# Pairs of units as one 1024-column product and one weighting, a third folded pair of quads, and a reordered prologue

## The chip, the cores and the metric

The kernel runs on one core of one Trainium2 chip. The metric is the device time of one execution in microseconds (us), the median of several runs. Engines are named as in the profile: PE (TensorE), DVE (VectorE), ACT (ScalarE), POOL (GpSimd) and SP (SyncE, which here only issues DMAs).

## The reference

x is 8 batches of 512 tokens of 256 features. Every batch goes through four layers in order, each adding to x:

- Layers 0 and 3: linear attention (16 and 8 heads) on a normalised x, with a softmax over the tokens for the keys and over a head's features for the queries; then y is normalised, scaled and shifted by the condition, passed through SiLU and projected.
- Layers 1 and 2: a state-space block on a normalised, modulated x, whose core is

```
def step(h, inp):
    dt_t, B_t, C_t, u_t = inp
    dA = jnp.exp(dt_t[:, :, None] * A)
    h = h * dA + (dt_t * u_t)[:, :, None] * B_t[:, None, :]
    y = jnp.einsum('bdn,bn->bd', h, C_t)
```

with 512 channels and 16 states for each channel, over 512 tokens. The result is multiplied by silu(z) and projected.

## The kernel before, in words

A **unit** is one state n of 128 channels: a scan along the 512 tokens, 128x512 elements. A scan (one batch, one of layers 1 and 2) has 4 chunks of 128 channels and 16 states, so 64 units, in two halves of 32: within a half the units run over n, and for each n over the half's two chunks. Those two successive units have the same row of B and the same row of C. There are 16 scans, so 1024 units.

A unit g consists of

- the decay exp(dt*A), by ACT;
- the injection dtu*B. For a unit of kind BESIDE, ACT writes the decay to one of three PSUM banks (L887) and POOL writes dtu*B into the unit's state slot (L664). For a unit of kind SPREAD, ACT writes the decay to SBUF (L903) and copies the row of B into a PSUM bank (L895), and DVE multiplies that bank by dtu in place (L1153);
- the scan on DVE (L1160 for BESIDE, L1163 for SPREAD), in place in one of 20 state slots. Before, unit g uses PSUM bank g % 3, free once unit g - 3 is scanned (`m_scan`);
- the weighting by the row of C on POOL, in place (L673, `weight`);
- the sum over n: PE adds the slot into a PSUM bank through the identity (L1463). Two of the eight quads (four units) of each half are not summed directly: an accumulating DMA issued by POOL (L677, `fold`) adds quad 0 into quad 1 and quad 3 into quad 4, and PE sums only the targets.

`KINDS` gives the kind: of 16 units, 7 are BESIDE. Rows of B and C come by DMA from SP into rings of four rows each, and a slot is free when the units that use it are done.

All engines walk one program order: a tick for each unit, in two parts, and in each part first the unit's own work and then as many steps of the chains (attention, the preparation of the next scan `before`, the work after a scan `after`, setup) as are due by hand-tuned tables of ticks (`ATT_STAGES`, `PREP_STAGES`, `POST_STAGES`, `TAIL_STAGES`, `SETUP_STAGES`). POOL also forms dtu = dt*u for each half of a scan (L629, 128x1024) and, by a power, the inverse roots of the norms (L605). Every engine works in order, so a chain's step that waits holds back the units behind it. Leads and lags in ticks: the row and the decay in a bank are made 2 ticks ahead, POOL's injection 3 ahead, the DVE product (L1153) 1 ahead of its scan, the weighting 2 behind, the sum 4 behind (12 for a folded quad).

Ahead of unit 0 lie the loads, attention 0, most of attention 1 and the preparation of scan 0. Among them the ACT queue waits, ahead of attention 0's normalisation, for the masks to have been stored to DRAM (L745), and DVE makes the masks and then the pieces of the biases (`bias_pieces`).

Of the kernel before, what the change touches and what calls it, by code (L numbers as in the profile page):

```python
# [34 lines left out]
KINDS = (BESIDE, SPREAD) * 7 + (SPREAD, SPREAD)  # L35
TAIL_UNITS, POST_END, PREP_END = 3, {1: 24, 2: 26}, 60
SETUP_UNITS, FIRST_PREP, FIRST_ATT = (-147, -66), (-79, -14), (-71, 34)
ATT_UNITS = ((32, 92), (93, 154), (154, 218), (218, 281))
# [25 lines left out]
MOD_PICK = 8 * DC + 2 * TT  # L64
MODS = MOD_PICK + 1
# [14 lines left out]
def by_name(names, durations):  # L80
# [4 lines left out]
    "first": (3, 19, 20, 20, 31, 13, 4, 6, 28, 4, 62, 1, 1, 2, 9, 13, 10, 15, 0, 2, 11, 15, 37, 4, 14, 6, 0, 2, 30,  # L85
              16, 10, 1, 18, 17, 29, 26, 34, 15, 65, 18, 9, 1, 11, 0, 10, 3, 12, 0, 20, 7, 4, 14),
    "second": (2, 1, 3, 2, 0, 4, 0, 3, 3, 4, 4, 2, 3, 3, 3, 0, 0, 4, 0, 2, 5, 14, 1, 22, 2, 0, 16, 3, 1, 0, 2, 0, 6,
# [9 lines left out]
    "last": (8, 7, 10, 2, 26, 4, 13, 17, 8, 24, 13, 58, 8, 11, 1, 12, 8, 4, 27, 33, 3, 6, 46, 2, 11, 1, 34, 2, 16, 11,  # L97
             12, 12, 5, 20, 5, 6, 6, 5, 60, 0, 20, 8, 12, 15, 5, 6, 22, 17, 4, 1, 3, 4),
})
PREP_STAGES = by_name(PREP_NAMES, {  # L100
    "first": (5, 9, 3, 1, 2, 3, 0, 4, 5, 3, 0, 4, 7, 4, 0, 1, 4, 5, 9, 1, 6, 9, 4, 9),
# [4 lines left out]
})  # L106
POST_STAGES = by_name(POST_NAMES, {
# [4 lines left out]
})  # L112
TAIL_STAGES = by_name(TAIL_NAMES, {
    0: (3, 14, 7),
    1: (0, 32, 4),
    2: (14, 7, 5),
    3: (34, 17, 9),
})
SETUP_STAGES = dict(zip(SETUP_NAMES, (0, 1, 1, 0, 15, 38, 1, 22, 3, 24, 3, 10), strict=True))
# [35 lines left out]

def kind_of(g):
    return KINDS[g % len(KINDS)]


def nth(g):  # L160

    kind = kind_of(g)
    return g // len(KINDS) * KINDS.count(kind) + KINDS[:g % len(KINDS) + 1].count(kind)
# [4 lines left out]

def spread_unit(n):
    return SPREAD_UNITS[n - 1]  # L170


def quad_of(g):
    return g // HALF_UNITS, g % HALF_UNITS // QUAD
# [154 lines left out]
def bass_cond_seq(nc, x, out, mask_cols, keep_cols, mask_rows0, mask_rows3, order, const_pack, att_packs, ssm_packs,  # L329
# [4 lines left out]
    with ctx:  # L334
# [583 lines left out]
        def _(dve):  # L918
# [112 lines left out]
            def attention(ai, layer, s, b):  # L1031
# [13 lines left out]
                if ai == 0:  # L1045
                    bias_pieces()
# [509 lines left out]
```

## Time and profile before

| | before |
|---|---|
| median of 3 runs | 2320.88 us (2319.4 to 2322.88) |
| profiled execution | 2320.92 us, span 2318.9 us |
| POOL busy | 2000.3 us (86%) |
| DVE busy | 1980.6 us (85%) |
| PE busy | 1931.7 us (83%) |
| ACT busy | 1691.9 us (73%) |
| mean granted clock | 0.928 |

Busy time is the union of an engine's instructions. Back-to-back records overlap by some 0.05 to 0.1 us, so what an instruction costs in a full queue is the distance from start to start, which is less than its mean duration. The share over the whole span mixes a prologue of 137 us, the 1024 units, and an end in which one attention runs alone.

### The profile page before, as it was taken

Reading aid. Unit: us, or ns where it says so; the run is one execution under the profiler, and the core shown is the slowest. Engines: PE = TensorE matmul, PEld = TensorE weight load, DVE = VectorE, ACT = ScalarE, POOL = GpSimd, SP = SyncE. Lnnn points to the kernel's source line nnn. Section 1 sums busy time; section 2 is a strip of 40 time slices with the busy share of each in tenths; the row PEclk is TensorE's granted clock in tenths of the full one; section 3 lists DMA queues with packets and bytes.
Section 4 is the critical chain, followed back from the end, with each engine's and each line's share of the span. In section 5 each row is a group of like instructions: output and inputs, shape, how many; then the busy total and the mean of one; then the engine's idle time right before and its main releaser. Section 6 shows DMA issues by size and latency. Waiting matters only on the chain. (4 is left out here: it accounts for less than half of the span.)

```text
span 2318.9 us, 23892 instructions
## 1 busy us (share of the span) xinstructions
PE 1931.7 (83%) x5712; PEld 984.9 (42%) x5712; DVE 1980.6 (85%) x2705; ACT 1691.9 (73%) x2677; POOL 2000.3 (86%) x1720
## 2 busy tenths in 40 slices
PE   6767779898888889889888979889898978778786
PEld 5433324445444444435444444435445443333353
DVE  4468888989989898998989898998989998898862
ACT  2476868697787869688787968778796867678642
POOL 0079998989899998999899998998999999999950
PEclk9887989899999999899999999999999999898997
DMA  6046565655455565555546565564556555565620
GB/s 229 1 135 170 157 181 143 181 155 161 145 166 167 153 191 155 164 166 153 159 143 180 160 178 158 159 174 142 160 157 180 163 157 180 161 175 162 173 77 19
DMA packets 170538, 358.84 MB, mean 155 GB/s; under 512 B 19528, under 2 KB 27936, under 8 KB 161696
## 3 DMA queue, kind: packets, MB, share of 16 engines
q1 hardware_dynamic: 151504, 275.38, 36.3%
q0 software_dynamic: 9216, 67.11, 15.5%
q10 hardware_dynamic: 9680, 14.83, 1.8%
q8 instruction: 47, 0.77, 0.1%
q14 instruction: 91, 0.75, 0.1%
HBM read 284.85 MB, written 5.29 MB: 125 GB/s over the span
## 5 line engine op out<-in xcount | busy, mean ns | idle before, releaser
L673 POOL TENSOR_TENSOR state<-state,c_rows 128x512 f32<-128x512 f32 x1024 | 1313.3, 1340 | 86.5 <-DVE state L1160 46.3
L1463 PE MATMUL bank<-state,const_sb 128*128 128x512 f32 x1536 | 766.7, 617 | 84.9 <-POOL state L673 78.8
L1163 DVE TENSOR_TENSOR_SCAN state<-decay,bank 128x512 f32<-128x512 f32 x576 | 687.8, 1203 | 18.9 <-ACT decay L903 17.6
L664 POOL TENSOR_TENSOR state<-kept,b_rows 128x512 f32<-128x512 f32 x448 | 589.5, 1316 | 0.1
L895 ACT ACTIVATE bank<-b_rows 128x512 f32<-128x512 f32 x576 | 342.3, 594 | 294.6 <-DVE state L1160 240.4
L1160 DVE TENSOR_TENSOR_SCAN state<-bank,state 128x512 f32<-128x512 f32 x448 | 544.1, 1215 | 7.8 <-POOL state L664 7.1
L1153 DVE TENSOR_TENSOR bank<-kept,bank 128x512 f32<-128x512 f32 x576 | 392.5, 681 | 113.4 <-ACT bank L895 110.4
L1463 PEld LDWEIGHTS bank<-state,const_sb 128*128 128x128 f32 x1536 | 282.3, 196 | 408.3 <-issue 210.4
L903 ACT ACTIVATE decay<-kept,ssm_pack 128x512 f32<-128x512 f32 x576 | 409.2, 710 | 2.7 <-issue 1.6
L887 ACT ACTIVATE bank<-kept,ssm_pack 128x512 f32<-128x512 f32 x448 | 304.0, 679 | 31.2 <-DVE state L1163 25.6
L1361 PE MATMUL bank<-kept,ssm_pack 128*128 128x512 f32 x512 | 256.7, 637 | 32.2 <-DVE kept L1113 14.5
L1264 PE MATMUL bank<-att_pack,xnT 128*128 128x256 f32 x768 | 246.1, 445 | 0.0
L1361 PEld LDWEIGHTS bank<-kept,ssm_pack 128*128 128x128 f32 x512 | 100.2, 204 | 160.0 <-issue 106.7
L1264 PEld LDWEIGHTS bank<-att_pack,xnT 128*128 128x128 f32 x768 | 144.1, 209 | 45.5 <-issue 13.3
L1417 PE MATMUL bank<-kept 128*128 128x256 f32 x512 | 138.6, 421 | 14.3 <-DVE kept L1128 14.3
L605 POOL TENSOR_TENSOR att_rstd<-att_var_eps,neg_half 128x4 f32<-128x4 f32 x32 | 33.9, 1058 | 127.2 <-DVE att_minus L1020 127.2
L1113 DVE SCALAR_TENSOR_TENSOR kept<-bank,ssm_pack,kept 128x511 f32<-128x511 f32 (+2 forms) x192 | 128.8, 739 | 16.4 <-ACT kept L828 16.3
L1417 PEld LDWEIGHTS bank<-kept 128*128 128x128 f32 x512 | 107.2, 214 | 50.4 <-issue 36.1
L1245 PE MATMUL bank<-const_sb,xn 128*128 128x128 f32 x384 | 63.7, 295 | 69.4 <-ACT xn L727 39.1
L629 POOL TENSOR_TENSOR kept<-kept 128x1024 f32<-128x1024 f32 x32 | 76.4, 2388 | 50.7 <-ACT kept L809 48.6
L1262 PE MATMUL bank<-bias_rows,right_rows 3*128 3x256 bf16 x192 | 56.1, 292 | 55.1 <-ACT kexp L761 20.3
L1245 PEld LDWEIGHTS bank<-const_sb,xn 128*128 128x128 f32 x384 | 46.9, 150 | 119.7 <-ACT xn L727 52.6
(144 smaller groups left out, 2090.3 us busy)
## 6 DMA issues: line engine op xcount, KB each, us to landing
b_rows<-flat_rows SPq DMA_DIRECT2D x512, 256.0 KB, 3.5
c_rows<-flat_rows SPq DMA_DIRECT2D x512, 256.0 KB, 3.3
state<-state POOLq DMA_DIRECT2D x64, 1024.0 KB, 8.3
out<-x_res ACTq DMA_DIRECT2D x8, 512.0 KB, 5.7
x_next<-x ACTq DMA_DIRECT2D x6, 512.0 KB, 4.8
kept<-film_w SPq DMA_DIRECT2D x2, 1024.0 KB, 12.7
ssm_pack<-ssm_pack SPq DMA_DIRECT2D x1, 2035.0 KB, 14.4
ssm_pack<-ssm_pack ACTq DMA_DIRECT2D x1, 2035.0 KB, 22.2
```

Source lines behind the costliest of these rows:

```text
L664: pool.tensor_tensor(state[:, g % STATES], dtu[:, c], b_rows[:, row % ROWS], ALU.mult).then_inc(m_inject[BESIDE], 1)
L673: pool.tensor_tensor(st, st, c_rows[:, row % ROWS], ALU.mult).then_inc(m_prod, 1)
L887: act.activation(mix_banks[g % BANKS][:], dt[:, c, :], ACT.Exp, scale=neg_a[scan_of(si)[0]][:, c * N + n:c * N + n + 1]).then_inc(m_decay[ ...
L895: act.activation(mix_banks[g % BANKS][:], b_rows[:, row % ROWS], ACT.Copy).then_inc(m_brow, 1)
L903: act.activation(decay[:, nth(g) % DECAYS, :], dt[:, c, :], ACT.Exp, scale=neg_a[scan_of(si)[0]][:, c * N + n:c * N + n + 1]).then_inc(m_d ...
L1153: dve.tensor_tensor(row[:], dtu[:, c, :], row[:], ALU.mult).then_inc(m_inject[SPREAD], 1)
L1160: ins = dve.tensor_tensor_scan(st, mixed, st, 0.0, ALU.mult, ALU.add)
L1163: ins = dve.tensor_tensor_scan(st, decay[:, nth(g) % DECAYS], mixed, 0.0, ALU.mult, ALU.add)
L1264: ins = pe.matmul(dst, lhs[:, c, t * P:(t + 1) * P], weights[:, c, :], start=(c == 0 and bias is None), stop=(c == DC - 1))
L1361: ins = pe.matmul(dst[:], w_in[:, c, (at + e) * P:(at + e + 1) * P], xnT_[:, c, :], start=(c == 0), stop=(c == DC - 1))
L1417: ins = pe.matmul(dst[:, (t % 2) * D:(t % 2 + 1) * D], lhs[:, c, t * P:(t + 1) * P], weights[:, c, :], start=(c == 0), stop=(c == CH - 1))
L1463: pe.matmul(y_banks[c2][:], ident, state[:, g % STATES], start=False, stop=(g == in_bank[-1])).then_inc(m_sum, 1)
```

## The change

- `kind_of` is now the kind of a pair of units (7 of 16 pairs BESIDE, so the share stays). POOL's injection and weighting, and DVE's product, are one instruction of 128x1024 for a pair, with the row of B or C read twice by a broadcast. ACT copies the row of B once for a SPREAD pair. DVE reads that bank for both chunks and writes the two neighbouring banks. `bank_plan` chooses the banks, now one PSUM tensor of three.
- `PRODUCT_LEAD` is 0: DVE's product of a pair stands directly ahead of its first scan and waits by `m_scan` for the bank's last scan. `SUM_LAG` is 5.
- `FOLDS` has three pairs: quad 0 into 1, 2 into 3, 4 into 5.
- The attention's scale, shift and SiLU are one ACT instruction with the Silu function; before, it was Identity and Tanh on ACT (L796, L797) and a product on DVE (L1086). POOL's three small copies per attention, preparation and end of a scan (L618, L640, L654) go, and so does ACT's row of gates (L871): PE takes a column of the identity instead.
- Prologue: x of batch 0 is loaded first, in halves by SP and ACT; DVE normalises before it makes masks; the masks' way through DRAM is on SP's queue alone; the large weights are issued behind it; keys wait only for their own bias; setup and the first chains have other start ticks.
- All tables of ticks have new values.

```
-BANK_LEAD, DECAY_LEAD, WEIGHT_LAG, SUM_LAG = 2, 2, 2, 4
+BANK_LEAD, DECAY_LEAD, WEIGHT_LAG, SUM_LAG = 2, 2, 2, 5
-INJECT_LEAD = 3
+INJECT_LEAD, PRODUCT_LEAD = 3, 0
-FOLDS = ((0, 1), (3, 4))
+FOLDS = ((0, 1), (2, 3), (4, 5))
-KINDS = (BESIDE, SPREAD) * 7 + (SPREAD, SPREAD)
-SETUP_UNITS, FIRST_PREP, FIRST_ATT = (-147, -66), (-79, -14), (-71, 34)
+KINDS = ((BESIDE, SPREAD) * 4 + (SPREAD,)) + ((BESIDE, SPREAD) * 3 + (SPREAD,))
+SETUP_UNITS, FIRST_PREP, FIRST_ATT = (-113, -84), (-94, -25), (-89, 34)
...
+def bank_plan():
+
+    freed, of_unit, of_row, scanned = {0: -3, 1: -1, 2: -2}, {}, {}, {}
+    for p in range(ALL_UNITS // HC):
+        first, second = sorted(freed, key=freed.get)[:HC]
+        if pair_kind(p) == SPREAD:
+            row = first or second
+            of_row[p], scanned["row", p] = row, freed[row]
+            first, second = row - 1, row
+        for g, k in ((p * HC, first), (p * HC + 1, second)):
+            of_unit[g], scanned[g] = k, freed[k]
+            freed[k] = g
+    return of_unit, of_row, scanned
...
@@ gpsimd: weight, inject
-                if c2 == 0:
-                    pool.wait_ge(c_loaded[row % ROWS], 16 * (si * (HALVES * N // ROWS) + row // ROWS + 1))
-                pool.wait_ge(m_scan, g + 1)
-                st = state[:, g % STATES]
-                pool.tensor_tensor(st, st, c_rows[:, row % ROWS], ALU.mult).then_inc(m_prod, 1)
+                pool.wait_ge(c_loaded[row % ROWS], 16 * (si * (HALVES * N // ROWS) + row // ROWS + 1))
+                pool.wait_ge(m_scan, g + HC)
+                st = pair_states(g)
+                pool.tensor_tensor(st, st, by_pair(c_rows[:, row % ROWS]), ALU.mult).then_inc(m_prod, 1)
...
-                state_free(pool, g - STATES)
-                pool.tensor_tensor(state[:, g % STATES], dtu[:, c], b_rows[:, row % ROWS], ALU.mult).then_inc(m_inject[BESIDE], 1)
+                for k in range(g, g + HC):
+                    state_free(pool, k - STATES)
+                pool.tensor_tensor(pair_states(g), dtu[:, c:c + HC], by_pair(b_rows[:, row % ROWS]),
+                                   ALU.mult).then_inc(m_inject[BESIDE], 1)
...
@@ vector: inject
-                dve.wait_ge(m_brow, nth(g))
-                row = mix_banks[g % BANKS]
-                dve.tensor_tensor(row[:], dtu[:, c, :], row[:], ALU.mult).then_inc(m_inject[SPREAD], 1)
+                past(dve, m_scan, BANK_FREED[g] + 1)
+                dve.wait_ge(m_brow, nth_pair(g // HC))
+                at, row = BANK_OF[g], ROW_BANK[g // HC]
+                both = mix[:, at:row + 1, :]
+                dve.tensor_tensor(both, dtu[:, c:c + HC, :], by_pair(mix_banks[row]), ALU.mult).then_inc(m_inject[SPREAD], 1)
...
@@ scalar: attention
-                    act.activation(xnT[:, c, :], pa[:], ACT.Identity, **args)
-                    act.activation(pa[:], pa[:], ACT.Tanh, **args).then_inc(a_hid, 1)
+                    act.activation(xnT[:, c, :], pa[:], ACT.Silu, scale=scale[:, c:c + 1],
+                                   bias=shift[:, c:c + 1]).then_inc(done, 1)
```

## Rows read from the trace of the kernel before

**Rows 1.** Busy time in one stretch, from first to last but a few units.

```profile
core 0: us, PE busy (x) PEld busy (x) DVE busy (x) ACT busy (x) POOL busy (x), PEclk, DMA share, GB/s
140.00:2215.00 2075.00, 1749.88 (x5000) 868.54 (x5000) 1883.44 (x2486) 1601.05 (x2521) 1963.45 (x1673) 0.93 0.58 164
```

**Rows 2.** Waits from 140 to 2215 us: total us, times, longest.

```profile
DVE bank L1153 <- ACT bank L895: 94.5, 92, 2.9
DVE state L1160 <- POOL state L664: 7.1, 12, 0.9
...
POOL state L673 <- DVE state L1163: 39.4, 31, 3.4
POOL state L673 <- DVE state L1160: 36.3, 27, 4.2
```

**Rows 3.** Groups by line: count | busy us, mean ns | idle before, releaser.

```profile
L673 POOL TENSOR_TENSOR state<-state,c_rows 128x512 f32<-128x512 f32 x1024 | 1313.3, 1340 | 86.5 <-DVE state L1160 46.3 <-DVE state L1163 39.4
L1463 PE MATMUL bank<-state,const_sb 128*128 128x512 f32 x1536 | 766.7, 617 | 84.9 <-POOL state L673 78.8 <-DMA state<-state 4.2
...
L895 ACT ACTIVATE bank<-b_rows 128x512 f32<-128x512 f32 x576 | 342.3, 594 | 294.6 <-DVE state L1160 240.4 <-DVE state L1163 32.5 <-DVE x_res L1090 12.2
...
L833 ACT ACT_TABLE_LOAD x32 | 41.1, 1283 | 0.6
...
L797 ACT ACTIVATE bank<-bank,mod_att 128x512 f32<-128x512 f32 x32 | 23.8, 742 | 0.0
...
L1086 DVE SCALAR_TENSOR_TENSOR xnT<-bank,xnT 128x512 f32<-128x512 f32 x32 | 21.6, 675 | 23.5 <-ACT bank L797 23.5
...
L1128 DVE TENSOR_TENSOR kept<-ssm_pack,bank 128x1024 f32<-128x1024 f32 x16 | 19.3, 1207 | 1.7 <-PE bank L1426 1.6
```

**Rows 4.** Timeline of POOL: start us, us, instruction.

```profile
400.81 2.35 POOL L629 TENSOR_TENSOR kept<-kept 128x1024 f32<-128x1024 f32 x1 [0.65 <-ACT kept L809]
403.12 1.27 POOL L673 TENSOR_TENSOR state<-state,c_rows 128x512 f32<-128x512 f32 x1
...
2190.87 2.52 POOL L673 TENSOR_TENSOR state<-state,c_rows 128x512 f32<-128x512 f32 x2
2193.32 1.30 POOL L664 TENSOR_TENSOR state<-kept,b_rows 128x512 f32<-128x512 f32 x1
2194.53 0.80 POOL L677 DMA_DIRECT2D state<-state  x1
2195.19 5.13 POOL L673 TENSOR_TENSOR state<-state,c_rows 128x512 f32<-128x512 f32 x4
```

**Rows 5.** Timeline of DVE: among the units, then in attention 0.

```profile
1505.16 0.67 DVE L1153 TENSOR_TENSOR bank<-kept,bank 128x512 f32<-128x512 f32 x1
1505.74 0.68 DVE L1090 TENSOR_TENSOR x_next<-bank,x_next 128x512 f32<-128x512 f32 x1
...
41.88 0.69 DVE L1063 TENSOR_REDUCE qstat<-bank 128x32 f32<-128x512 f32 x1 [0.15 <-PE bank L1264]
42.60 0.70 DVE L1064 TENSOR_TENSOR bank<-bank,qstat 128x512 f32<-128x512 f32 x1
```

**Rows 6.** Timeline of ACT around a change of table.

```profile
1188.27 0.71 ACT L903 ACTIVATE decay<-kept,ssm_pack 128x512 f32<-128x512 f32 x1
1188.99 1.28 ACT L848 ACT_TABLE_LOAD   x1
1190.29 1.09 ACT L848 ACTIVATE kept<-bank 128x512 f32<-128x512 f32 x2
```

**Rows 7.** The prologue: ACT, PE, DVE; then line L1163 with median ns and starts.

```profile
26.91 0.60 ACT L727 ACTIVATE xn<-x_next,att_shift,att_rstd 128x256 f32<-128x256 f32 x1 [20.66 <-DMA mask_adds<-decay]
...
33.28 3.68 PE L1251 MATMUL bank<-xnT,att_pack 128*128 128x512 f32 x4 [0.96 <-ACT xnT L755]
...
137.01 1.22 DVE L1160 TENSOR_TENSOR_SCAN state<-bank,state 128x512 f32<-128x512 f32 x1
...
L1163 DVE TENSOR_TENSOR_SCAN state<-decay,bank x576: 1192/1197/1221, 138.1 to 2231.6; 128x512 f32<-128x512 f32 x192
```

More of the change, by code:

```diff
@@ L291, in timeline @@
         if si < SCANS:
-            chains.append(Chain(tail(si, *scan_of(si)), ticks(TAIL_STAGES[si % SLOTS]), at, at + TAIL_UNITS))
+            chains.append(Chain(tail(si, *scan_of(si)), ticks(TAIL_STAGES[si % SLOTS]),
+                                at if si > 0 else max(at, FIRST_PREP[1]), at + TAIL_UNITS))
         if si > 0:
@@ L486, in state_free, with pair_states, by_pair @@
                 eng.wait_ge(m_sum, SUM_COUNT[g])
+        def pair_states(g):
+            return state[:, g % STATES:g % STATES + HC, :]
+        def by_pair(row):
+            return row.unsqueeze(1).broadcast_to([P, HC, T])
         def quad_states(half, quad):
@@ L562, in used @@
             def used(si, g):
-                first = si * UNITS + HC * g
-                for k in range(first, first + HC):
-                    if kind_of(k) == BESIDE:
-                        past(sp, m_inject[BESIDE], nth(k))
-                    if kind_of(k) == SPREAD:
-                        past(sp, m_brow, nth(k))
+                p = si * HALVES * N + g
+                if pair_kind(p) == BESIDE:
+                    past(sp, m_inject[BESIDE], nth_pair(p))
+                if pair_kind(p) == SPREAD:
+                    past(sp, m_brow, nth_pair(p))
             def feed(si, parity):
@@ L680, in unit @@
             def unit(g, part):
-                if part == 0 and is_unit(g - WEIGHT_LAG):
-                    weight(g - WEIGHT_LAG)
+                last = g - WEIGHT_LAG
+                if part == 0 and is_unit(last) and last % HC == HC - 1:
+                    weight(last + 1 - HC)
                 if part == 0:
                     return
-                if is_unit(g + INJECT_LEAD) and kind_of(g + INJECT_LEAD) == BESIDE:
-                    inject(g + INJECT_LEAD)
+                first = g + INJECT_LEAD
+                if is_unit(first) and first % HC == 0 and kind_of(first) == BESIDE:
+                    inject(first)
                 for n, (source, into) in enumerate(FOLDS):
@@ L818, in before @@
                 yield from w.to("xT")
-                act.wait_ge(p_mod, pi + 1)
+                scale, shift = mod_cols(b, MOD_AT[layer], DC), mod_cols(b, MOD_AT[layer] + DC, DC)
+                if b == 0:
+                    act.wait_ge(s_mod[layer], 1)
                 for c in range(DC):
                     bank_, done = filled(act, prep_fill(pi, f"turn{c}"))
-                    act.activation(prep_xnT[s][:, c, :], bank_[:], ACT.Identity, scale=mod_prep[:, c:c + 1],
-                                   bias=mod_prep[:, DC + c:DC + c + 1]).then_inc(done, 1)
+                    act.activation(prep_xnT[s][:, c, :], bank_[:], ACT.Identity, scale=scale[:, c:c + 1],
+                                   bias=shift[:, c:c + 1]).then_inc(done, 1)
                 for first in (0, 2):
@@ L866, in after @@
                 w = Walk(stages)
-                if qi > 0:
-                    taken(act, post_fill(qi - 1, "gate"))
-                act.wait_ge(s_gate_nat, 2)
-                act.wait_ge(o_pick, qi + 1)
-                act.activation(gate_row, gate_nat[:, layer - 1, :], ACT.Copy, scale=gate_pick[on_gates, :]).then_inc(o_row, 1)
                 if layer == 2:
@@ L907, in unit @@
                 if part == 0:
-                    if is_unit(g + BANK_LEAD):
-                        (b_row_in_bank if kind_of(g + BANK_LEAD) == SPREAD else decay_in_bank)(g + BANK_LEAD)
+                    ahead = g + BANK_LEAD
+                    if is_unit(ahead) and kind_of(ahead) == BESIDE:
+                        decay_in_bank(ahead)
+                    if is_unit(ahead) and kind_of(ahead) == SPREAD and ahead % HC == 0:
+                        b_row_in_bank(ahead)
                     return
@@ L1081, in attention @@
                 moments(att_norm, y, a_var, link)
-                for c in range(DC):
-                    yield from w.to(f"act{c}")
-                    dve.wait_ge(a_hid, ai * DC + c + 1)
-                    pa, done = att_bank(ai, f"yT{c}")
-                    dve.scalar_tensor_tensor(xnT[:, c, :], pa[:], 1.0, xnT[:, c, :], ALU.add, ALU.mult).then_inc(done, 1)
                 for h in range(2):
@@ L1177, in unit @@
                 if part == 0:
-                    if is_unit(g + 1) and kind_of(g + 1) == SPREAD:
-                        inject(g + 1)
+                    first = g + PRODUCT_LEAD
+                    if is_unit(first) and first % HC == 0 and kind_of(first) == SPREAD:
+                        inject(first)
                     return
```

192 lines of the change are left out of this document (94 added, 98 removed), and 34 rows, old and new, of tables (ATT_STAGES, POST_STAGES, PREP_STAGES).

## The prediction

> **What bounds the kernel now.** I first read the busy times of the stretch from 140 to 2215 us, which is the 1024 units without prologue and end [rows 1]. POOL works 1963 of 2075 us (94.6%), DVE 1883 (90.8%), PE 1750 (84%), ACT 1601 (77%). Then the waits in the same stretch [rows 2]: POOL waits for DVE's scans 76 us, DVE waits for POOL's injections only 7 us, and DVE's largest wait is for the row of B in its bank, 94.5 us in 92 waits. So POOL is nearly full, DVE is close behind it, and the two meet with little slack. A gain must come off POOL first, and it ends where DVE is full. The reader should see that nothing can be read from the shares of the whole span: 86% and 85% look alike, and the stretch tells them apart.
>
> The profiled execution took 2320.92 us, 2.0 more than its span and equal to the median of 2320.88, so the sum below is made on it and carried over as it is. A difference under 0.2% (4.6 us) is no more than the runs before differ among themselves.
>
> **POOL.** Two 512-column weightings take 2.45 us from start to start (2190.87 to 2193.32), and the one form of 1024 columns that POOL runs now takes 2.31 (400.81 to 403.12) [rows 4]. It has two SBUF inputs and an SBUF output like the new ones; only the repeated row is new. I take 2.31. There will be 1024/2 weightings and 448/2 injections of pairs, 736 in all: 736 x 0.14 = 103 us less. Bounds: 0 if the repeated row costs what was saved, and 736 x 0.2 = 147 if the overlap of records is larger than in this row. The third fold is 32 more issues by POOL, each 0.66 us from its start to the next one's (2194.53 to 2195.19) [rows 4]: +21. The small copies that go are worth a few us, set at nothing. POOL's work in the stretch: 1963 - 103 + 21 = 1881 us.
>
> **DVE.** (1) The product of the attention's SiLU goes: 32 x 0.58 (0.675 less the overlap) = 19 us less [rows 3]. (2) The product of a pair: before 2 x 0.58 us (1505.16 to 1505.74) [rows 5]; the nearest 1024-column product with a PSUM input takes 1.21 [rows 3], some 0.09 of it overlap, so 1.12. 288 pairs x 0.04 = 12 us less. (3) The new waits. Before, the product stood one unit ahead of its scan, with another scan between them. Now the product waits for the scan just ahead of it (that scan's bank is the one it writes, in nearly all SPREAD pairs by the plan of banks), and the next scan waits for the product. An instruction that needs its predecessor starts 0.03 us after its record's end (41.88 + 0.69, then 42.60), one that doesn't starts 0.09 ahead of it (1505.16 + 0.67, then 1505.74) [rows 5]: 0.12 us for each such wait, two in each of 288 pairs, 69 us. A chain's work in between hides one; I count about 23 groups of chain work on DVE in the 128 half-ticks of a scan, a sixth, so 57 us. The Trainium skill (VectorE: DVE Perf Modes, The DRAIN you can't avoid) says the contrary: chained copies with a semaphore after each took as long as with one at the end, so these waits would be free, and term (3) would be 0 instead of 57. The trace here speaks against it. Bounds of (3): 0 and 69. DVE: 1883 - 19 - 12 + 57 = 1909 us. DVE is then the fuller engine.
>
> **The slack between them.** DVE is idle for 192 us of the stretch. 94.5 of it is the wait for the row of B [rows 2]. ACT's copy can start when the scan three units back is done, and the product wanted it after one more scan; now it wants it after two more, since the product moved back by a unit, and ACT makes one copy per pair instead of two. I take that wait away. 1909 + 97 = 2006. POOL by its own idle of 112 would give 1881 + 112 = 1993. I take 2008: 67 us less than 2075.
>
> **ACT** loses 288 copies at about 0.54 each, 156 us, and 24 us of Tanh [rows 3]. But Tanh runs without a load of its own, while each stretch of Silu among the exponentials costs a table load (L833: 32 loads) [rows 3], and another one for the next exponential. With the two SiLUs of an attention apart, that is up to 4 loads x 16 = 64; from the load's start to the next start is 1.30 us [rows 6], so up to 83 us. ACT ends near 1601 - 156 - 24 + 83 = 1504 us, far from full, so in the sum it is nothing; its cover is ACT's idle 474 us and the lead of two ticks. Without cover it is the second rival below.
>
> **PE** sums 20 units of a half instead of 24: 128 sums, 256 instructions less [rows 3], at about 0.43 us each 110 us. PE is 84% busy and not the bound; it makes the chains arrive earlier. The folds' transfers (1 MB each) go from 64 to 96, the busy share of the DMA engines from 0.58 [rows 1] to some 0.66. The rows of B and C are asked for four pairs ahead, some 16 us; nothing is charged. That every sum is a tick later, and a half's last sums one tick too, shifts the gate, not the rate.
>
> **Prologue.** Attention 0's normalisation starts on ACT at 26.91, after 20.66 us of waiting for the masks to reach DRAM, and keys at 33.28 [rows 7]. Afterwards x comes first, and normalised x should stand near 12 us. But the keys still need the masks and the key bias, and DVE makes these now behind the statistics: I put them at 18, which is 15 us earlier. The products of the condition no longer lie in the gap ahead of the keys but among the attention's own; their matmuls fit its idle time. On the other side the preparation's order ahead of the first scan (137.01) [rows 7] is little changed. Taken: -15; bounds -25 and -3. SP's queue now waits for the masks twice ahead of the state-space weights of layer 1; they are wanted by the preparation only, after 80 us.
>
> **End.** From the last scan (2231.6) [rows 7] to the end are 87 us of sums, projection and the last attention, alone. Identity, Tanh and product become one load and two SiLUs, and fewer sums stand in PE's queue: -2.
>
> Sum: 2320.9 - 67 - 15 - 2 = **2237 us**.
>
> **The rivals.**
> A. *Free waits, tighter coupling.* If term (3) is 0, DVE needs 1852 and POOL with 1881 stays the bound: 1993 with POOL's present idle, which is 2222. If the looser leads also take idle time off POOL as they do off DVE (its 76 us of waiting for scans halved), 1955, which is 2184. For it: in 92 waits DVE is held by a bank, and POOL's waits follow from them. Against it: the 0.12 us. Its middle is 2203.
>
> B. *The chains take it back.* Table loads sit in ACT's queue directly ahead of decays. If half of the 64 hold up a scan, 32 x 1.3 = 42 us return: 2279. For it: ACT's 0.7 us decays have two ticks of lead, and a load with two SiLUs is 3 us. Against it: such loads stand in the queue now, and DVE waits little for decays. The Trainium skill (ScalarE: Activation LUTs, What ACT_TABLE_LOAD costs) gives a drain of about 1.38 us beside the 1.28 of the load; this trace shows no such drain, since the load starts as the instruction before it ends. By the page the same half would be 85 us, and the time 2322.
>
> C. *Slower: POOL and DVE hold each other.* On an odd tick t POOL weights the pair that ended at t-2, then injects the pair at t+3. Between the end of scan t-2 and the start of scan t+3 DVE has four scans and a pair's product, about 4 x 1.13 + 1.12 + 0.24 = 5.9 us. POOL has two 1024-column products in it, 4.6 us; before it was 2.45 in 5.7. So slack falls from 3.2 to 1.3 us, and the 2.31 us of dt*u, a root (about 1.2) or a fold in that window leave DVE waiting. To reach the time before, the 224 BESIDE pairs must each wait 84/224 = 0.37 us on average; at 0.5 us (112 us) the time is 2349. For it: each engine's window is now a pair wide. Against it: DVE waits for injections 7 us in all, and the other chain work on DVE widens the window.
>
> **How the numbers follow.** Forecast (2220 to 2260) 0.58, A 0.17, B 0.18, C 0.07. The forecast is its own sum. The range takes in A and B but for their far ends: 2185 to 2290, which leaves out C, the lowest of A and the highest of B, together under 0.2. Faster by over 0.2%: forecast, A and nearly all of B, 0.91; within 0.2%: 0.02; slower: 0.07.
>
> **What would show it.** POOL's pair products at 2.3 us from start to start and POOL's work near 1881 in the stretch; DVE's product followed by its scan with a gap of 0.03 us instead of an overlap; DVE's wait for the row of B nearly gone; DVE's share of the stretch above POOL's; about 64 table loads more; keys of attention 0 before 20 us and the first scan near 122. The prediction is wrong if the pair product on POOL takes 2.45 or more (then some 100 us come back and only the prologue is left), if L1160's successor waits for POOL's injection by tens of us (C), or if the waits for decays grow (B).

## The result, and the profile after

The changed kernel takes 2380.81 us (median; 2379.54 to 2381.71) where the kernel before, run beside it, takes 2321.88: 1.025 times as long, with an interval of 1.0233 to 1.0266. The forecast was 2237. The profiled execution has a span of 2379.9 us against 2318.9, 61.0 more.

The page of the kernel after, its first part (busy us, share, instructions):

```profile
PE 1908.6 (80%) x5456; PEld 961.3 (40%) x5456; DVE 1973.9 (83%) x2378; ACT 1597.8 (67%) x2403; POOL 1927.5 (81%) x970
```

The 61 us split at the first scan and at the last one. The first scan starts at 141.31 instead of 137.01 (+4.3; forecast -15), the stretch of the units takes 2145 instead of 2095 (+50; forecast -67), and what lies behind the last scan 93.4 instead of 87.3 (+6.1; forecast -2). Busy time in the units' stretch, from the first scan to the last, of the kernel before:

```profile
core 0: us, PE busy (x) PEld busy (x) DVE busy (x) ACT busy (x) POOL busy (x), PEclk, DMA share, GB/s
137.00:2232.00 2095.00, 1764.12 (x5038) 875.34 (x5038) 1900.51 (x2505) 1615.12 (x2543) 1981.72 (x1688) 0.93 0.58 163
```

and of the kernel after:

```profile
core 0: us, PE busy (x) PEld busy (x) DVE busy (x) ACT busy (x) POOL busy (x), PEclk, DMA share, GB/s
141.00:2286.00 2145.00, 1733.36 (x4750) 847.42 (x4749) 1899.89 (x2190) 1514.17 (x2266) 1906.56 (x942) 0.89 0.63 175
```

POOL works 75 us less, DVE the same, ACT 101 less. Their idle time grew instead: POOL's from 113 to 238 us, DVE's from 194 to 245. DVE's work is the same in both, so the 50 us of the stretch are DVE's idle time. The granted clock of the whole profiled execution is 0.888 instead of 0.928.

The waits after, from 140 to 2260 us (us in total, times, longest):

```profile
ACT mix_banks L913 <- DVE state L1185: 241.4, 120, 9.4
POOL state L695 <- DVE state L1185: 138.3, 89, 4.0
...
PE bank L1489 <- DMA state<-state: 122.5, 38, 9.5
...
DVE kept L1197 <- PE bank L1489: 72.3, 27, 7.4
DVE state L1185 <- ACT decay L929: 59.3, 40, 6.2
```

L1489 is PE's sum, L1197 the gate that takes the finished sum out of its bank, L695 POOL's weighting, L1185 the SPREAD scan, L929 its decay. The wait of 94.5 us for the row of B [rows 2] is down to 11.3, as forecast. PE now stands for a fold's transfer (122.5 us; in the kernel before 4.2 [rows 3]), and DVE's gates stand for PE (72.3; in the kernel before 10.2 from the first scan to the last). Groups by line after (busy, mean ns | idle before, releasers):

```profile
L695 POOL TENSOR_TENSOR state<-state,c_rows 128x1024 f32<-128x1024 f32 x512 | 1233.4, 2451 | 187.3 <-DVE state L1185 140.0 <-DVE state L1182 46.8
L1489 PE MATMUL bank<-state,const_sb 128*128 128x512 f32 x1280 | 700.5, 668 | 163.7 <-DMA state<-state 128.8 <-POOL state L695 34.4
```

One such wait on the timelines, from POOL's issue of a fold to PE's sums (start us, us, instruction, [idle before]):

```profile
452.53 0.88 POOL L699 DMA_DIRECT2D state<-state  x1 [0.30 <-POOL state L695]
...
462.19 7.29 PE L1489 MATMUL bank<-state,const_sb 128*128 128x512 f32 x16 [0.91 <-DMA state<-state]
```

The transfer lands 9.7 us after its issue, and sixteen matmuls leave the moment it has. PE stood 0.91 us for it here; the longest of these waits is 9.5 us. A second place, where the gate is the one that stands:

```profile
534.78 2.04 PE L1489 MATMUL bank<-state,const_sb 128*128 128x512 f32 x2 [3.64 <-DMA state<-state]
...
550.87 0.69 DVE L1197 TENSOR_TENSOR kept<-bank,kept 128x512 f32<-128x512 f32 x1 [5.21 <-PE bank L1489]
```

The prologue, with keys of attention 0 on PE, and at the end of it the first scan on DVE:

```profile
24.85 3.62 PE L1275 MATMUL mix_banks<-xnT,att_pack 128*128 128x512 f32 x4 [11.58 <-DMA right_rows<-mask_adds]
...
140.96 0.42 DVE L1097 TENSOR_TENSOR att<-bank,att_pack 128x256 f32<-128x256 f32 x1 [23.23 <-PE bank L1330]
141.31 2.33 DVE L1182 TENSOR_TENSOR_SCAN state<-mix_banks,state 128x512 f32<-128x512 f32 x2
```

### The profile page after: what moved, and what is told of

The parts are those of the page before. It is cut to its first block and busy times, and to the rows that moved or that the text cites. A ratio compares the mean times of both kernels' runs of the same rounds, so it can differ in the third digit from the quotient of the medians.

```text
span 2379.9 us, 21432 instructions
## 1 busy us (share of the span) xinstructions
PE 1908.6 (80%) x5456; PEld 961.3 (40%) x5456; DVE 1973.9 (83%) x2378; ACT 1597.8 (67%) x2403; POOL 1927.5 (81%) x970
## 5 line engine op out<-in xcount | busy, mean ns | idle before, releaser
L695 POOL TENSOR_TENSOR state<-state,c_rows 128x1024 f32<-128x1024 f32 x512 | 1233.4, 2451 | 187.3 <-DVE state L1185 140.0
L1489 PE MATMUL bank<-state,const_sb 128*128 128x512 f32 x1280 | 700.5, 668 | 163.7 <-DMA state<-state 128.8
L1185 DVE TENSOR_TENSOR_SCAN state<-decay,mix_banks 128x512 f32<-128x512 f32 x576 | 678.4, 1209 | 80.0 <-ACT decay L929 59.3
L1182 DVE TENSOR_TENSOR_SCAN state<-mix_banks,state 128x512 f32<-128x512 f32 x448 | 526.5, 1203 | 29.7 <-ACT mix_banks L913 20.0
L686 POOL TENSOR_TENSOR state<-kept,b_rows 128x1024 f32<-128x1024 f32 x224 | 544.1, 2429 | 2.0 <-issue 2.0
L913 ACT ACTIVATE mix_banks<-kept,ssm_pack 128x512 f32<-128x512 f32 x448 | 303.6, 682 | 254.1 <-DVE state L1185 249.9
L1489 PEld LDWEIGHTS bank<-state,const_sb 128*128 128x128 f32 x1280 | 258.3, 214 | 479.4 <-issue 333.2
L929 ACT ACTIVATE decay<-kept,ssm_pack 128x512 f32<-128x512 f32 x576 | 390.6, 710 | 3.4 <-ACT x_dbl L868 2.0
L1175 DVE TENSOR_TENSOR mix_banks<-kept,mix_banks 128x1024 f32<-128x1024 f32 x288 | 352.8, 1225 | 18.3 <-ACT mix_banks L921 11.3
L921 ACT ACTIVATE mix_banks<-b_rows 128x512 f32<-128x512 f32 x288 | 171.4, 595 | 148.4 <-DVE state L1185 132.0
L1359 PE MATMUL bank<-x_dbl,ssm_pack 64*128 64x512 f32 x128 | 93.5, 868 | 22.4 <-ACT x_dbl L868 22.4
L1197 DVE TENSOR_TENSOR kept<-bank,kept 128x512 f32<-128x512 f32 x64 | 43.4, 677 | 81.7 <-PE bank L1489 81.7
```

What stands on the lines that cost most here:

```text
L686: pool.tensor_tensor(pair_states(g), dtu[:, c:c + HC], by_pair(b_rows[:, row % ROWS]), ALU.mult).then_inc(m_inject[BESIDE], 1)
L695: pool.tensor_tensor(st, st, by_pair(c_rows[:, row % ROWS]), ALU.mult).then_inc(m_prod, 1)
L913: act.activation(mix_banks[BANK_OF[g]], dt[:, c, :], ACT.Exp, scale=neg_a[scan_of(si)[0]][:, c * N + n:c * N + n + 1]).then_inc(m_decay[BE ...
L921: act.activation(mix_banks[ROW_BANK[g // HC]], b_rows[:, row % ROWS], ACT.Copy).then_inc(m_brow, 1)
L929: act.activation(decay[:, nth(g) % DECAYS, :], dt[:, c, :], ACT.Exp, scale=neg_a[scan_of(si)[0]][:, c * N + n:c * N + n + 1]).then_inc(m_d ...
L1175: dve.tensor_tensor(both, dtu[:, c:c + HC, :], by_pair(mix_banks[row]), ALU.mult).then_inc(m_inject[SPREAD], 1)
```

## Experiments

Each ratio is to the kernel before run beside it. The expectations go by letters for what the cost could be. F, P and T stood first: the third fold; the pairs, which couple the engines too closely; the new tick tables. Then P was split: O, the order of kinds by pairs; D, DVE's product at no lead; W, POOL's pair instructions, whose results come later. L came last: the loop of DVE and ACT through the three banks sets the pace, and POOL only fills the time beside it.

### The third fold and the tables

Taking the third fold out of the changed kernel:

```
-FOLDS = ((0, 1), (2, 3), (4, 5))
+FOLDS = ((0, 1), (3, 4))
```

> The changed kernel with the folds of before (quad 0 into 1, quad 3 into 4); pairs, tables and prologue stay. Theory F (the third fold is the cause: its target is summed last of a half, PE waits 122 us for fold transfers, and DVE's gates wait 72 us for PE): those waits go below 20 us each, and the time falls by 60 to 90 us, to about 2300. Theory P (the pairs themselves couple the engines too closely: ACT waits 380 us for scans, POOL 185 us): the time falls by less than 20 us, since PE's wait was beside other work. Theory T (the new tables of ticks fit badly): under 20 us too.

Measured 2342.82, ratio 1.0086 (1.0071 to 1.0101): 38 us back of the 59. PE's wait for transfers is gone from the list of waits. In its place stands PE's wait for POOL's weightings (from 145 to 2240 us, 111.9 us in 41 waits), and POOL's own wait for the SPREAD scans is 153.4 us. The time fell by less than the 60 to 90 us that F asked and by more than the 20 that P or T allowed: the fold is part of the cost, and the rest is still slower than before.

The changed kernel with the tick tables of before, with three folds and with two (the rows of the tables are too long to print):

```
 # ATT_STAGES "A" to "last", PREP_STAGES 0 to 3, POST_STAGES, TAIL_STAGES: before's rows
-TAIL_UNITS, POST_END, PREP_END = 3, {1: 26, 2: 25}, 60
+TAIL_UNITS, POST_END, PREP_END = 3, {1: 24, 2: 26}, 60
-ATT_UNITS = ((31, 96), (97, 154), (154, 219), (221, 287))
+ATT_UNITS = ((32, 92), (93, 154), (154, 218), (218, 281))
```

> The changed kernel with the tables of ticks of before for all that comes behind the prologue (attentions from the third on, preparations from the second, work after a scan, tails, and where they start and end). Theory T: the time falls by 40 us or more. Theory F: no change within 10 us, with the waits for fold transfers still above 100 us. Theory P: within 15 us either way.

> Both of the above together: the changed kernel with two folds and the tables of before. What is left of the change is pairs, the Silu instruction and the prologue. By the blind sum with its two engines' work this should be near 2250 if F and T hold together; by theory P it stays above 2330.

Measured 2483.33, ratio 1.0689 (1.0673 to 1.0705), and 2377.15, ratio 1.023 (1.0212 to 1.0248). The new tables save 102 us with three folds and 34 with two. T is refuted, and no theory had the 102 us. It is also a first sign of how much the written order alone moves.

The third fold put into the kernel before, the first edit the other way round (`FOLDS = ((0, 1), (2, 3), (4, 5))`):

> The kernel before with three folds (quad 0 into 1, 2 into 3, 4 into 5) and nothing else. Theory F: slower than before by 40 us or more, with the waits of PE for fold transfers and of the gates for PE that the changed kernel has. Theories P and T: within 20 us of before, since the fold needs the pairs or the tables to hurt.

Measured 2409.18, ratio 1.0374 (1.0356 to 1.0393): 87 us slower. Its waits from 145 to 2220 us, with L1463 the sum and L1174 the gate:

```profile
DVE kept L1174 <- PE bank L1463: 72.1, 28, 6.6
PE bank L1463 <- DMA state<-state: 71.9, 20, 10.6
```

So the third fold is dear in either kernel, as F had it: 38 us in the one, 87 in the other.

### The rest, one part at a time

The kernel before with its kinds dealt by pairs, and nothing else:

```
-KINDS = (BESIDE, SPREAD) * 7 + (SPREAD, SPREAD)
+KINDS = ((BESIDE, SPREAD) * 4 + (SPREAD,)) + ((BESIDE, SPREAD) * 3 + (SPREAD,))
 def kind_of(g):
-    return KINDS[g % len(KINDS)]
+    return pair_kind(g // HC)
```

> The kernel before with the kinds dealt out by pairs of units (7 of 16 pairs BESIDE) and every instruction still of one unit. Work of each engine is the same; only the order changes: two BESIDE units in a row want two injections from POOL and two decays in banks together, two SPREAD units two copies and two DVE products together. Theory O (the order by pairs is itself a cost): slower than before by 15 us or more. Theory D (it is DVE's product of a pair, which hangs between two scans) and theory W (it is POOL's pair instructions, whose results come later): within 8 us of before.

Measured 2356.59, ratio 1.0158 (1.013 to 1.0186): 36 us slower for the order by pairs. One wait on DVE grew by about as much, that of the product (here L1162) for the row of B, 94.5 us in the kernel before [rows 2]; from 145 to 2220 us:

```profile
DVE bank L1162 <- ACT bank L904: 128.4, 92, 7.2
```

On top of it POOL's instructions by pairs:

```
-                pool.tensor_tensor(st, st, c_rows[:, row % ROWS], ALU.mult).then_inc(m_prod, 1)
+                pool.tensor_tensor(st, st, by_pair(c_rows[:, row % ROWS]), ALU.mult).then_inc(m_prod, 1)
...
-BANK_LEAD, DECAY_LEAD, WEIGHT_LAG, SUM_LAG = 2, 2, 2, 4
+BANK_LEAD, DECAY_LEAD, WEIGHT_LAG, SUM_LAG = 2, 2, 2, 5
```

> The same and POOL's injection and weighting as one 1024-column instruction for a pair, sums one tick later (5) as in the change; DVE and ACT as before. POOL's work falls by about 100 us. My blind sum would have this faster than the kernel with kinds by pairs by some 60 us. Theory W: no faster than it, or slower, with POOL's time given back in waits for scans.

Measured 2397.86, ratio 1.0335 (1.0312 to 1.0359): 41 us slower again, although POOL works 98 us less in all (1907.0 instead of 2005.4). Its waits for scans grew from 88 to 193 us, as W had it.

From the other end: the changed kernel with two folds, with DVE's product and ACT's copy per unit again and a lead of one unit:

```
-INJECT_LEAD, PRODUCT_LEAD = 3, 0
+INJECT_LEAD, PRODUCT_LEAD = 3, 1
...
-                dve.tensor_tensor(both, dtu[:, c:c + HC, :], by_pair(mix_banks[row]), ALU.mult).then_inc(m_inject[SPREAD], 1)
+                dve.tensor_tensor(row, dtu[:, c, :], row, ALU.mult).then_inc(m_inject[SPREAD], 1)
...
-                act.activation(mix_banks[ROW_BANK[g // HC]], b_rows[:, row % ROWS], ACT.Copy).then_inc(m_brow, 1)
+                act.activation(mix_banks[g % BANKS], b_rows[:, row % ROWS], ACT.Copy).then_inc(m_brow, 1)
```

> The changed kernel with two folds (2342.8 us), in which DVE's product and ACT's copy of the B row are of one unit again: banks in turn (unit mod 3), the product one unit ahead of its scan. POOL's pairs stay. Theory D: faster by 20 us or more, to 2320 or below, as 2 x 0.12 us of waits in each SPREAD pair go; DVE's busy time rises by some 12 us, ACT's by 150. Theories W and O: within 10 us, or slower, since ACT has twice the copies to make.

Measured 2440.69, ratio 1.0512 (1.0484 to 1.054), 98 us slower than with the pair product; DVE's product waits 205.5 us for the row of B (from 145 to 2260 us). D is refuted: DVE's pair product, ACT's single copy and the plan of banks are together a large gain in this order; the run does not tell them apart. And with POOL's products per unit again:

```
-                pool.tensor_tensor(st, st, by_pair(c_rows[:, row % ROWS]), ALU.mult).then_inc(m_prod, 1)
+                pool.tensor_tensor(st, st, c_rows[:, row % ROWS], ALU.mult).then_inc(m_prod, 1)
```

> The changed kernel with two folds (2342.8 us), in which POOL's injection and weighting are of one unit again; DVE's pair product stays. POOL's work rises by about 100 us. Theory W: the time is the same or lower, since each result comes 1.1 us earlier. Theories D and O: slower by 20 to 60 us, as POOL's pairs were a real saving.

Measured 2342.89, ratio 1.0094 (1.0074 to 1.0114), beside 2342.82 with pairs. The pages of the two, with pairs and with units:

```profile
PE 1932.6 (83%) x5712; PEld 982.0 (42%) x5712; DVE 1974.2 (84%) x2378; ACT 1598.1 (68%) x2403; POOL 1898.3 (81%) x938
PE 1925.9 (82%) x5712; PEld 983.0 (42%) x5712; DVE 1976.6 (84%) x2378; ACT 1599.1 (68%) x2403; POOL 1996.2 (85%) x1674
```

POOL works 98 us more and the time is the same: the saving on which the forecast was built is worth nothing here, which is theory W again.

The mirror of it, all that is not pairs, third fold or steady tables (prologue, SiLU in place of Tanh and product, the dropped copies, the gates by PE), put into the kernel before. As a diff to the changed kernel:

```
-FOLDS = ((0, 1), (2, 3), (4, 5))
+FOLDS = ((0, 1), (3, 4))
-KINDS = ((BESIDE, SPREAD) * 4 + (SPREAD,)) + ((BESIDE, SPREAD) * 3 + (SPREAD,))
+KINDS = (BESIDE, SPREAD) * 7 + (SPREAD, SPREAD)
-BANK_LEAD, DECAY_LEAD, WEIGHT_LAG, SUM_LAG = 2, 2, 2, 5
+BANK_LEAD, DECAY_LEAD, WEIGHT_LAG, SUM_LAG = 2, 2, 2, 4
...
```

> The change without its pairs and its third fold: units, kinds, banks, leads, sums and steady tables of ticks as before; prologue (with its own tables), the Silu instruction, the dropped copies and the gates by PE as in the changed kernel. If pairs and the third fold are all that costs, this is at or below the time before: 2300 to 2320. If the rest costs too (a prologue 4 us later, table loads), 2325 to 2345.

Measured 2351.85, ratio 1.0138 (1.0121 to 1.0155): 33 us slower, more than either case expected. First scan at 143.9, last at 2263.2, so 7 us lie in the prologue and 25 in the units; waits for decays went from 16.3 to 44.9 us. (Products, copies and banks are per unit and the steady tables those of before, as in the edits above.) These edits stood in tables made for other edits, so the 33 us are theirs only in this company.

The attention's table loads, in the changed kernel with two folds. This kernel computes another function than the reference, and only its time is of use:

```
-                    act.activation(xnT[:, c, :], pa[:], ACT.Silu, scale=scale[:, c:c + 1],
+                    act.activation(xnT[:, c, :], pa[:], ACT.Tanh, scale=scale[:, c:c + 1],
```

> The changed kernel with two folds (2342.8 us), in which the attention's last activation computes tanh in place of SiLU, so that it needs no table load of its own. Some 29 loads before it and as many behind it go, 58 x 1.3 = 75 us of ACT's work. By my rival B (half of the loads hold up a scan) the time falls by 20 to 40 us; if ACT's idle time hides them, by less than 8.

Measured 2333.39, ratio 1.0035 (1.0019 to 1.005) against 1.0086: 0.5%, about 12 us. ACT has 57 loads less and works 74 us less. This is the second rival's price: real, and some quarter of the 42 us that rival asked.

### What each engine's work is worth in the kernel before

Each of these leaves out some columns of one kind of instruction in an otherwise unchanged kernel, so that one engine loses work and the results are no longer the reference's. The work taken out is read from the pages: the engine's busy time against the kernel before.

```
+                pool.tensor_tensor(st[:, 0:464], st[:, 0:464], c_rows[:, row % ROWS, 0:464], ALU.mult).then_inc(m_prod, 1)
...
+                dve.tensor_tensor(row[:, 0:352], dtu[:, c, 0:352], row[:, 0:352], ALU.mult).then_inc(m_inject[SPREAD], 1)
...
+                act.activation(mix_banks[g % BANKS][:, 0:320], b_rows[:, row % ROWS, 0:320], ACT.Copy).then_inc(m_brow, 1)
...
+                pe.matmul(y_banks[c2][:, 0:384], ident, state[:, g % STATES, 0:384], start=False, stop=(g == in_bank[-1])).then_inc(m_sum, 1)
```

> The kernel before, in which POOL's weighting leaves out the last 48 of a unit's 512 columns (they stay unweighted): POOL's work falls by about 1024 x 0.11 = 113 us, as much as the pairs were to save, with every wait and order as it is. Theory L (the loop of DVE and ACT through the three banks sets the pace and POOL only fills the time beside it): the time falls by less than 30 us. My prediction's reading (POOL, 94.6% busy, is the bound): it falls by 60 us or more.

> The kernel before, in which DVE's product for SPREAD units leaves out the last 160 columns: DVE's work falls by 576 x 0.167 = 96 us. Theory L: the time falls by 50 us or more, although DVE is busy for less of the time than POOL. My prediction's reading: less than 20 us, since POOL stays the bound.

> The kernel before, in which ACT's copy of the row of B leaves out the last 192 columns (the bank keeps what it held): ACT's work falls by 576 x 0.16 = 92 us, and each copy is ready 0.16 us earlier. Theory L: the time falls by 30 us or more though ACT is idle for a quarter of the time, as the copy lies in the loop from one scan to the product three units on. My prediction's reading: under 10 us.

> The kernel before with the three cuts together (48 columns less in POOL's weighting, 160 in DVE's product, 192 in ACT's copy), whose single effects were 15, 27 and 18 us. If each engine's queue adds its own part to a shared loop, the effects add: about 60 us, to 2262. If one engine takes over as the bound when another is relieved, together they give much more than the sum: 90 us or more (POOL's 113 and DVE's 96 less what PE then holds).

> The kernel before, in which PE sums only the first 384 of 512 columns of a unit: PE's work falls by a quarter of 768 sums, about 768 x 0.21 = 160 us. If PE's in-order queue is a part of what delays the chains, the time falls by 15 us or more; if its idle time covers it, under 8.

```
cut of              work taken out   time       ratio (interval)            us back   share
POOL, 48 columns    100 us           2309.91    0.9932 (0.9909 to 0.9955)   15.8      16%
DVE, 160 columns     88 us           2297.35    0.9882 (0.9867 to 0.9897)   27.4      31%
ACT, 192 columns     76 us           2306.32    0.9914 (0.9893 to 0.9935)   20.0      26%
all three           277 us           2237.68    0.9638 (0.9615 to 0.9661)   84        30%
PE, 128 columns      93 us           2329.85    1.0047 (1.0031 to 1.0063)   -11
```

(us back is one less the ratio, times the 2324.73 or, for the last two, 2319.08 of the kernel before.) No engine is the bound: each gives back a sixth to a third of what it saves, and ACT, with 474 idle us before, gives back more for each us than POOL with 112. The prediction's reading (POOL 60 us or more, DVE under 20, ACT under 10) fails in all three, and theory L (DVE 50 or more, ACT 30 or more) in two. The three together give back 84, more than the 63 of the single cuts added and less than the 90 of a bound that passes from one engine to the next. The rest is the order: an engine that is done earlier waits for a neighbour that isn't. With DVE's cut, DVE works 88 us less from the first scan to the last and stands 64 more (259 for 194): for the row of B 121 instead of 97, for decays 28 instead of 18, and for POOL's injections 14 instead of 7. The last row is taken up in the last section.

### The lag of the folded sums

If the third fold's cost is PE standing ahead of a transfer that has not landed, a sum later by two ticks should free it. In the changed kernel:

```
-FOLDED_LAG = 12
+FOLDED_LAG = 14
```

> The changed kernel (2380.8 us) with its three folds, and the sums of folded quads 14 ticks behind instead of 12. Theory F in detail (PE stands in front of the last fold's transfer and the gates wait for PE): PE's wait for transfers falls below 60 us, but the gates come two ticks later in order, and the time falls by 10 to 30 us. If the transfers themselves are the cost (their load on DMA and POOL's queue), it stays within 8 us.

Measured 2317.30, ratio 0.9992 (0.998 to 1.0005): 63 us less than the changed kernel, where 10 to 30 were expected, and the time of the kernel before. The stretch of the units:

```profile
core 0: us, PE busy (x) PEld busy (x) DVE busy (x) ACT busy (x) POOL busy (x), PEclk, DMA share, GB/s
139.00:2220.00 2081.00, 1667.35 (x4752) 835.92 (x4751) 1899.63 (x2190) 1514.32 (x2266) 1905.46 (x942) 0.91 0.66 180
```

Against the changed kernel's row the work of DVE, ACT and POOL is the same to about 1 us, PE's busy time is 66 us less for the same matmuls at a clock of 0.91 for 0.89, and the stretch is 64 us shorter. The waits that went, from 145 to 2180 us:

```profile
PE bank L1489 <- DMA state<-state: 47.3, 16, 7.3
...
DVE kept L1197 <- PE bank L1489: 12.9, 6, 5.5
```

The gate's wait fell by 59 us (to 13.5 from the first scan to the last) and DVE's whole idle time by 64. The same edit in the kernel before with three folds (`FOLDED_LAG = 14`):

> The kernel before with three folds (2409.2 us) and folded sums 14 ticks behind instead of 12. If the third fold costs by its place in PE's queue only, most of its 87 us come back: 2320 to 2340. If it costs by its transfers and POOL's issues too, it stays above 2350.

Measured 2406.44, ratio 1.0367 (1.0345 to 1.0389), against 1.0374 without it. The gate's wait fell as it should, from 72.1 to 13.7 us, and the time did not follow; PE's wait for the normalised x stands at 95.9 us. DVE's idle time fell by 13 us only (279 to 267; 194 in the kernel before), since its wait for the row of B rose from 104 to 119 and small waits for PE in the chains took most of the rest. So in that order the lag is not what costs.

Last, attention 1 later in the prologue of the version with lag 14, to take its work out of the way of the first decay:

```
-SETUP_UNITS, FIRST_PREP, FIRST_ATT = (-113, -84), (-94, -25), (-89, 34)
+SETUP_UNITS, FIRST_PREP, FIRST_ATT = (-113, -84), (-94, -25), (-71, 34)
```

> The changed kernel with folded sums 14 ticks behind (2317.3 us), and attention 1 started at tick -71 as before instead of -89, so that less of it stands in the queues ahead of unit 0. In the changed kernel DVE waits 23.2 us, until 140.8, for that attention's product, with the first scan right behind it. If that is the prologue's loss, the first scan comes at 130 to 136 instead of 139 and the time is 2308 to 2314, faster than both kernels; if the attention's work only moves in among the units and costs there, the time stays within 4 us of 2317.

Measured 2350.47, ratio 1.0114 (1.0089 to 1.0138): slower, with the first scan at 163.3. The expectation had the wrong sign. ACT's queue ahead of the first decay and DVE's first scan, first in the changed kernel, then here:

```profile
136.52 0.60 ACT L816 ACTIVATE kexp<-bank 128x512 f32<-128x512 f32 x1 [0.81 <-PE bank L1269]
137.14 1.28 ACT L913 ACT_TABLE_LOAD   x1
138.43 1.30 ACT L913 ACTIVATE mix_banks<-kept,ssm_pack 128x512 f32<-128x512 f32 x2
```

```profile
160.59 0.60 ACT L816 ACTIVATE kexp<-bank 128x512 f32<-128x512 f32 x1 [1.26 <-PE bank L1269]
161.21 1.28 ACT L913 ACT_TABLE_LOAD   x1
162.50 1.30 ACT L913 ACTIVATE mix_banks<-kept,ssm_pack 128x512 f32<-128x512 f32 x2
...
163.28 2.34 DVE L1182 TENSOR_TENSOR_SCAN state<-mix_banks,state 128x512 f32<-128x512 f32 x2 [23.70 <-ACT mix_banks L913]
```

The edit did not take attention 1 out of the way: its copies still stand directly ahead of the first decay in ACT's queue, only 24 us later. No version run without leaving work out is faster than the kernel before by more than the measurement can tell.

## Why the prediction was wrong

**The work of POOL, DVE and ACT: right.** POOL's was to change by -103 + 21 = -82 and changed by -75 (1981.7 to 1906.6): over the whole span the pairs took off 98 (the two pages above) and the small copies some 4, and the third fold added 29 instead of 21 (1898.3 to 1927.5). DVE's recorded work was to fall by 19 + 12 and rise by the overlaps lost to the new waits (the 0.09 of each 0.12; the other 0.03 is a gap, recorded as idle), 43 of the 57: +12. It changed by -1. ACT's was to change by -97 and changed by -101, with 248 table loads instead of 186, 62 more for the 64. PE's was to fall by 110 and fell by 31 (1764.1 to 1733.4), as the last section shows; the sum had it at nothing.

**Term (3), the waits of product and scan: mechanism right, size a little above.** A SPREAD pair on DVE's timeline after:

```profile
1205.23 1.22 DVE L1182 TENSOR_TENSOR_SCAN state<-mix_banks,state 128x512 f32<-128x512 f32 x1
1206.49 1.23 DVE L1175 TENSOR_TENSOR mix_banks<-kept,mix_banks 128x1024 f32<-128x1024 f32 x1
1207.80 2.53 DVE L1185 TENSOR_TENSOR_SCAN state<-decay,mix_banks 128x512 f32<-128x512 f32 x2
```

The product starts 0.04 us after the scan's record ends and the scan 0.08 after the product's, instead of an overlap of 0.09: 0.13 and 0.17 us, not 0.12 twice. Over the whole trace, 218 of the 288 products follow a scan directly and 240 stand directly ahead of one, with medians of 0.03 us behind the scan and 0.09 ahead of the next: 218 x 0.12 + 240 x 0.18 = 69 us, for the 57 charged. By the measurement of chained copies in the Trainium skill (VectorE: DVE Perf Modes, The DRAIN you can't avoid) such waits would cost nothing; these rows do not agree.

**"The slack between them": the step that failed.** It took DVE's idle time down from 192 to 97 us, since the wait for the row of B would go, and so made the stretch of DVE's work and that idle (2006 us; it took 2008 and gave no reason for the 2). The wait did go (94.5 to 11.3), and the idle time came back under other names, 245 us in all for the 97: 72.3 us at the gate, 59.3 for decays (17.6 in the kernel before), 20 and 8 ahead of the BESIDE scans. Behind the step stood its reading of the profile: POOL is nearly full, DVE next, so a saving counts in full until the next engine is full. The cuts refute it. In the kernel before, 100 us off POOL are worth 15.8 and 88 off DVE 27.4; in the changed kernel with two folds POOL's whole saving of 98 us is worth nothing. 94.6% busy looked like a bound; the remaining 5.4% is where all the dependences between five queues are kept, and an engine at 77% returned more per us.

**"Nothing is charged" for the folds, and "shifts the gate, not the rate": the second failure.** The transfer was weighed against bandwidth (0.58 to 0.66 of the DMA engines; measured 0.63), not against the time at which its sum stands in PE's queue. The fold takes 9.6 us to land (median over L699; 8.3 in the kernel before, 8.5 there with three folds), PE is in order, and what stood behind that sum were attention's matmuls and the half's last sums, and behind those DVE's gates. Two more ticks of lag took 59 us off the gate's wait and 63 off the time, with every instruction the same. That is shown for this order of work, but for the share that the higher clock may have in it. That the gate's wait need not be a loss in itself is shown as well: in the kernel before with three folds the lag removed the same wait and the time stayed.

**What pairs cost in order.** In the prediction the pairs changed the lengths of instructions, and rival C alone had more. They also set the kinds of units in twos, and this alone cost the kernel before 36 us, and POOL's instructions by pairs another 41: a weighting now waits for two scans, and its waits for DVE rose from 88 to 193 us. This is kin to the first half of rival C, but not at its place: the scans wait 8.1 us for POOL's injections. DVE's own pair product, whose waits were charged at 57, was worth 98 to the kernel together with ACT's single copy and the plan of banks. The row of B copied once looks like the gain (205.5 us of waiting when it is copied per unit); no run separates it.

**The rivals.** A needed free waits; they are not. B's mechanism is there, at about 12 us instead of 42. The Tanh run took 74 us off ACT, 1.30 for each of its 57 loads, and there is no gap beside a load either: in the kernel before, 167 of 186 are followed by the next instruction within 0.1 us. The Trainium skill (ScalarE: Activation LUTs, What ACT_TABLE_LOAD costs) adds a drain of 1.38 us to each load; neither number agrees. C's sign was right and its mechanism wrong.

**Prologue: forecast -15, measured +4.3.** Keys came at 24.85, 8.4 us earlier, not 15: the keys wait for the masks' way through DRAM (11.58 us in the row above). The gain is then lost: the last wait ahead of the first scan is 23.23 us of an attention's bank from PE, and the first decay on ACT comes at 138.43, behind copies of attention 1. To start attention 1 later made it worse (163.3), with the same copies ahead of the first decay: that ACT's order holds the first scan back agrees with both, but no run put the copies behind the decay, and that stays open.

**End: forecast -2, measured +6.1.** A gate there waits 9.45 us for PE's sums; with lag 14 the end is 91.7.

**Open.** What costs 87 us in the kernel before with the third fold, when not the lag: POOL's 31 us more of work (2031.5 for 2000.3) and the clock of 0.89 for 0.93 are the visible differences. Why the order by pairs alone costs 36: the longer wait for the row of B goes with it, but no run tests it. And how much of either a table made for it would return: tables moved the time by 34 and 102 us, so no part's price here holds outside its own order.

## What to carry to other kernels

Where several engines are 77 to 95% busy under a written order, the fullest need not be the bound: before promising a saving, cut some 100 us from each engine in turn and read what comes back (here 16 to 31%). Count the hand-offs that a change makes wider, and when each arrives, as carefully as its work. Whatever lands by DMA needs its lag in an in-order queue set by the time to landing (9.6 us here): two ticks more of it were worth 63 us in one order of work, with not an instruction saved, and 3 in another.

## What the runs showed of the hardware that was not expected

Less work on PE came with a lower granted clock. The sums of 384 instead of 512 columns in the kernel before, otherwise the same:

```profile
L1463 PE MATMUL bank<-state,const_sb 128*128 128x384 f32 x1536 | 626.6, 525 | 114.8 <-POOL state L673 103.3 <-DMA state<-state 9.8 <-DVE v L1077 0.6
```

And PE's part of the page:

```profile
PE 1838.4 (79%) x5712; PEld 1016.4 (44%) x5712; DVE 1980.3 (85%) x2705; ACT 1691.3 (73%) x2677; POOL 1999.5 (86%) x1720
```

A quarter of the columns went, but the mean only from 617 [rows 3] to 525 ns, 15% less; the clock's mean fell from 0.928 to 0.894, and the kernel was 0.47% slower. Neither case of the expectation had it slower. The sums took 140 us less (766.7 to 626.6) and PE in all only 93 (1931.7 to 1838.4): its other matmuls, the chains' own, are busy for 1307 us by themselves instead of 1262, at the same count. In the changed kernel too, 256 sums less saved 66 us (766.7 to 700.5), not the 110 charged, at 668 ns each and 0.888, and the other matmuls are busy for 1290 us (1266 with two folds). The third fold in the kernel before takes them from 1262 to 1295. With lag 14, where PE stands less for transfers, the same sums take 633 ns at 0.910. The three-fold versions of the kernel before have 0.889 and 0.890. Of the clock's two levels, 1.2 and 2.4 GHz, a mean of 0.928 is 14% of the time at the lower one, and 0.888 is 22%. All runs with fewer sums or columns lie between 0.872 and 0.910, and all with the full sums between 0.907 and 0.934. That the clock is a cause of the longer time, and not only its companion, no run here separates.
